# Residual rows written by a scatter in stage one and loaded per block; the order of GpSimd's scatters

## The chip, the core and the metric

One core of a Trainium2 chip. The metric is the device time of one launch, in microseconds (us). TensorE (PE) multiplies, VectorE (DVE) and ScalarE (ACT) work on tiles, GpSimd (POOL) does small tiles and issues the indirect DMAs, and SyncE (SP) issues the plain DMAs from its own queue. Every engine runs its own list in order and waits on semaphores.

## What is computed

x has 8 sequences of 2048 tokens with 256 features, 16384 tokens in all.

```
x = x + layernorm(attention(layernorm(x)))     # RWKV: k, v, r projections, a log-space scan, output product
h2 = layernorm(x)
x = x + layernorm(moe(h2))                     # 8 experts, the best 2 of each token, plus a shared expert
```

`moe` weighs the two routed experts' outputs by the softmax of their logits and adds the shared expert's output, gated by a sigmoid. The last line needs three things for each token: the sum of its expert outputs, its shared expert's row, and the residual x as it stood before the experts.

## The kernel before

**Stage one** runs over NCH = 32 chunks of 512 tokens (NT = 4 tiles of 128 rows). The chunks go through a software pipeline that is written out by hand: every engine has a loop over i, and in turn i it handles chunk i in one function, chunk i-1 in the next, down to chunk i-6. What matters here, by chunk m:

- ACT, in its turn m+3, at the end: `squares_o(m)` (L731) and, later in the same turn, `squares_h2(m)` (L742), which need `residual(m)` of DVE (L1014).
- ACT, in its turn m+4: `h2_normed(m)` (L715) writes the normalised rows h2n. It waits for `scale_h2(m)` (L527) of POOL, which makes rstd and nb.
- PE, in its turn m+3, at the end: `T2(m)` transposes h2n. In its turn m+4 it does the output product of chunk m+1, `router_product(m)` and `gate_up_product(m)`; ACT's `gate(m)` (L770) evacuates the latter.
- ACT, in its turn m+5, as the last thing of the turn: `shared_out(m)` (L665) writes the shared expert's rows `ysh`.
- POOL, in its turn i: `scale_o(i-4)`, `scatter(i-5, 0)` and `scatter(i-5, 1)` (four indirect DMAs each, from h2n to the DRAM tensors d_xd0 and d_xd1, sorted by expert), `scale_h2(i-4)`, `scale_in(i)`, and last `shared_scatter(i-6)` (L554, four indirect DMAs, from ysh to d_xs). So the rows of `shared_out(m)` leave in POOL's turn m+6, at its end.

A scattered row carries, beside its 256 features, the weights, positions and token number, and in two more columns (`ext`) the factor and the mean from which the residual can be had back from the normalised row.

**Between the stages** SP writes zero blocks (`tails`, `shared_tails`, `tail_2`) behind the last row of every expert in each scattered tensor, DVE computes the block tables, and the last scatters land.

**Stage two** runs over 142 blocks of 256 rows, 71 for the first choice of each token and 71 for the second. SP loads the block (`load_block`) and, LY = 5 steps later, the result rows to add to (`load_result`: d_xs in the first half, d_ys in the second). PE transposes and multiplies, ACT and DVE split operands into high and low parts, DVE adds in `y_out` (L1327). In the first half POOL scatters the sums to d_ys. In the second half `back` (L1336) recomputes the residual on DVE from the block, `last_squares` (ACT, L887) and `last_scale` (POOL, L594) make the last norm's factor, `final` (DVE, L1345) puts them together and `tokens_out` (POOL, L605) scatters the rows to `out`.

POOL's order in stage one is this:

```
if on(i - 4): scale_o(i - 4)
if on(i - 5): scatter(i - 5, 0); scatter(i - 5, 1)
if on(i - 4) and i - 4 != NCH - 1: scale_h2(i - 4)
if 0 < i < NCH: scale_in(i)
if on(i - 6): shared_scatter(i - 6)
```

Of the kernel before, what the change touches and what calls it, by code (L numbers as in the profile page):

```python
# [14 lines left out]
P = 128  # L15
# [9 lines left out]
def rwkv_moe(nc, x, decay, u_in, mix_k, mix_v, mix_r, wkT, wvT, wrT, woT, router, w1, w2,  # L25
# [18 lines left out]
    NEXT = XW - C_EXT  # L44
# [6 lines left out]
    LY = 5  # L51
# [7 lines left out]
    d_xs = nc.dram_tensor("d_xs", [E * CAP + BLK, D], F32).ap()  # L59

    d_ys = nc.dram_tensor("d_ys", [E * CAP + BLK, D], F32).ap()

    with ExitStack() as ctx:
# [41 lines left out]
        x1 = sb("x1", [P, NT, D])  # L105
# [4 lines left out]
        lowf = sb("lowf", [P, P])  # L110
# [13 lines left out]
        sqo = sb("sqo", [P, 2, 2, D], BF16)  # L124
# [22 lines left out]
        ext = sb("ext", [P, 2, NT, NEXT])  # L147
# [12 lines left out]
        ioti = sb("ioti", [P, NBP], I32)  # L160
# [48 lines left out]
        s_ex = sem("s_ex")  # L209
        s_exc = sem("s_exc")  # L210
# [55 lines left out]
        s_zt = sem("s_zt")  # L266
        s_tb = sem("s_tb")
# [26 lines left out]
        s_back = sem("s_back")  # L294
# [17 lines left out]
        def rows(t):  # L312
# [11 lines left out]
              for i in range(2) for t in (kk, vv, tr, dl, nx, x1)]  # L324
# [8 lines left out]
        tbf = flat(hf)[:, 0:4 * NBP].rearrange("p (k s b) -> p k s b", k=2, s=2)  # L333
        stf = st[:, :, :, :].rearrange("p k a t -> p (k a t)")
# [4 lines left out]
        bigj = [t[:, 0:E * NJ].rearrange("p (e b) -> p e b", e=E) for t in room]  # L339

# [16 lines left out]
        def _(sp):  # L357
# [20 lines left out]
            def tails():  # L378

                sp.wait_ge(s_zt, 2)  # L380
                for s in range(2):
                    sp.dma_start(d_xd[s][E * CAP:E * CAP + BLK, :].rearrange("(p j) d -> p j d", p=P), zt
                                 ).then_inc(s_tail, 16)
                sp.dma_start(d_xs[E * CAP:E * CAP + BLK, :].rearrange("(p j) d -> p j d", p=P), zt[:, :, 0:D]
# [21 lines left out]
            sp.dma_start(x1[:, :, :], x_v[0]).then_inc(s_xr, 16)  # L406
            for i in range(NCH + 4):
# [18 lines left out]
            sp.wait_ge(s_tail, 16 * (E + 2))  # L426
# [3 lines left out]
            def load_block(b):  # L430
# [4 lines left out]
                first_row[b % (LY + 1)] = r  # L435
# [3 lines left out]
            def load_result(w):  # L439
# [4 lines left out]
                sp.dma_start(yb[w % NYB], rows_in[bass.ds(first_row[w % (LY + 1)], BLK), :].rearrange("(p j) d -> p j d", p=P)  # L444
                             ).then_inc(s_yl[w % NYB], 16)

            for b in range(NB + LY):
                if b == NB1:
                    sp.wait_ge(s_tab, 5)
                    sp.wait_ge(s_tail2, 16 * E)  # L450
# [6 lines left out]
                if b >= LY:  # L457
                    if b == LY:
                        sp.wait_ge(s_scy, 16 * NT * NCH)
                        sp.wait_ge(s_tail3, 16 * (E + 1))  # L460
                    if b - LY == NB1:
                        sp.wait_ge(s_tail4, 16 * (E + 1))
                        for w in range(NB1 - NYB, NB1):
                            sp.wait_ge(*landed(w))
                    load_result(b - LY)
# [5 lines left out]
        def _(pool):  # L471
            g = nc.gpsimd
            g.memset(ident[:, :], 0.0).then_inc(s_const, 1)
            g.memset(lowf[:, :], 1.0).then_inc(s_const, 1)
# [3 lines left out]
            g.affine_select(out=lowf[:, :], in_=lowf[:, :], compare_op=ALU.is_gt, fill=0.0,  # L478
# [5 lines left out]
            g.memset(ext[:, :, :, :], 0.0).then_inc(s_const, 1)  # L484
            g.memset(oneb[:, :], 1.0).then_inc(s_const, 1)
            g.memset(ones8[:, :], 1.0).then_inc(s_const, 1)
            g.iota(ioti[:, :], [[1, NBP]], base=0, channel_multiplier=0).then_inc(s_const, 1)
# [21 lines left out]
            def scale_in(c):  # L509
                if c:  # L510
                    pool.wait_ge(s_nx, n(c - 1, NT, NT))
                if c >= 4:
# [3 lines left out]
                    pool.wait_ge(s_ex, n(c - 4, 2, 2))  # L516
# [10 lines left out]
            def scale_h2(m):  # L527
# [8 lines left out]
                if m >= 2:  # L536
                    pool.wait_ge(s_exc, m - 1)
                g.tensor_tensor(ext[:, m % 2, :, 0], var[:, 2, :], rstd[:, 2, :], ALU.mult).then_inc(s_ex, 1)
                g.tensor_copy(ext[:, m % 2, :, 1], nmx[:, m % 4, :]).then_inc(s_ex, 1)

            def scatter(m, s):
                if s == 0:
                    pool.wait_ge(s_h2, n(m, NT, NT))
                    pool.wait_ge(s_ex, n(m, 2, 2))
                    g.tensor_copy(h2n_of(m)[:, :, C_EXT:XW], ext[:, m % 2, :, :]).then_inc(s_exc, 1)
                    pool.wait_ge(s_exc, m + 1)
                pool.wait_ge(s_pl, n(m, NPL, L_DST))
                pool.wait_ge(s_wt, n(m, NWT, W_CW))
                for j in range(NT):
                    k = s * NT + j  # L550
                    g.indirect_dma_start(d_xd[s], bass.IndirectOffsetOnAxis(ap=ixs[:, m % 2, k:k + 1], axis=0),  # L551
                                         h2n_of(m)[:, j, :], None).then_inc(s_sct, 16)

            def shared_scatter(m):  # L554
                pool.wait_ge(s_pl, n(m, NPL, L_IX))
                for j in range(NT):
                    pool.wait_ge(s_ys, n(m, NT, j + 1))
                    g.indirect_dma_start(d_xs, bass.IndirectOffsetOnAxis(ap=ixs[:, m % 2, j:j + 1], axis=0),  # L558
# [3 lines left out]
            for i in range(NCH + 6):  # L562
# [9 lines left out]
                if i - 4 == NCH - 1:  # L572
                    scale_h2(i - 4)
                if on(i - 5):
# [6 lines left out]
                if on(i - 6):  # L581
                    shared_scatter(i - 6)
# [39 lines left out]
        def _(act):  # L622
# [92 lines left out]
            def h2_normed(m):  # L715
# [8 lines left out]
                for j in range(NT):  # L724
                    A.activation(h2n_of(m)[:, j, 0:D], x1[:, j, :], ACT.Identity, bias=nb[:, 2, j:j + 1],
# [5 lines left out]
            def squares_o(m):  # L731


                if m:
                    act.wait_ge(s_va[1], m)
                for j in range(NT):
                    act.wait_ge(s_O, n(m, 2, j // 2 + 1))
                    if n(m, NT, j) >= 2:
                        act.wait_ge(s_sqo, n(m, NT, j) - 1)
                    A.activation(sqo[:, 0, j % 2, :], o_tile(j), ACT.Square, accum_out=sq[:, 0, j:j + 1]).then_inc(s_sqo, 1)  # L740
# [900 lines left out]
```

## Time and profile before

| | us |
|---|---|
| median of 3 runs | 1677.63 (1674.99 to 1678.86) |
| the profiled execution | 1681.43 |
| its span, first to last instruction | 1679.7 |

Busy shares over the span, from the page: PE 91%, DVE 84%, ACT 78%, POOL 66%. The granted clock's mean is 0.964. The slices of the page:

```profile
PE   4899999999999999999999996669999988888882
POOL 1156677677677677677667767535666647777776
PEclk9999999999999999999999998779999999999997
DMA  3113223222222222222322211389877745665561
```

Each digit is a fortieth of the span, 42 us. Stage one fills slices 1 to 26, stage two the rest. The busy time of a matmul is modelled, so "PE busy" tells that PE was never without work, not that it was at its peak. In the rows of a timeline, the bracket at the end is how long the engine was idle before the row, and what released it; "issue" is time for which the profile shows no release. A row may merge several equal instructions (x4).

### The profile page before, as it was taken

Reading aid. Unit: us, or ns where it says so; the run is one execution under the profiler, and the core shown is the slowest. Engines: PE = TensorE matmul, PEld = TensorE weight load, DVE = VectorE, ACT = ScalarE, POOL = GpSimd, SP = SyncE. Lnnn points to the kernel's source line nnn. Section 1 sums busy time; section 2 is a strip of 40 time slices with the busy share of each in tenths; the row PEclk is TensorE's granted clock in tenths of the full one; section 3 lists DMA queues with packets and bytes.
Section 4 is the critical chain, followed back from the end, with each engine's and each line's share of the span. In section 5 each row is a group of like instructions: output and inputs, shape, how many; then the busy total and the mean of one; then the engine's idle time right before and its main releaser. Section 6 shows DMA issues by size and latency. Waiting matters only on the chain.

```text
span 1679.7 us, 35120 instructions
## 1 busy us (share of the span) xinstructions
PE 1532.7 (91%) x9960; PEld 1373.8 (82%) x9960; DVE 1407.1 (84%) x3210; ACT 1314.1 (78%) x2699; POOL 1103.0 (66%) x1167
## 2 busy tenths in 40 slices
PE   4899999999999999999999996669999988888882
PEld 3778888888888888888888885668999988878872
DVE  4799998998998898899899888547777769999994
ACT  3788888898898898888898888545777767777772
POOL 1156677677677677677667767535666647777776
PEclk9999999999999999999999998779999999999997
DMA  3113223222222222222322211389877745665561
GB/s 119 39 52 92 98 82 101 98 85 93 91 85 84 87 85 84 91 82 76 102 80 77 90 66 66 111 263 294 253 238 245 240 155 162 200 213 174 185 206 62
DMA packets 122316, 214.42 MB, mean 128 GB/s; under 512 B 19975, under 2 KB 62730, under 8 KB 122128
## 3 DMA queue, kind: packets, MB, share of 16 engines
q1 hardware_dynamic: 90064, 126.13, 25.2%
q0 software_dynamic: 32064, 86.04, 14.1%
q8 instruction: 86, 1.41, 0.4%
q14 instruction: 102, 0.84, 0.2%
HBM read 116.37 MB, written 99.39 MB: 128 GB/s over the span
## 4 chain that ended last, share of the span: by engine, by line
PE 66%; POOL 7%; DVE 7%; issue 7%; DMA 4%; SPq 2%; ACT 2%; DVEq 1%; POOLq 0%; ACTq 0%
PE PS L1401 47%; PE PS L1581 6%; PE PS L1597 5%; PE PS L1393 3%; POOL out L609 2%; PE PS L1464 2%; POOL d_ys L591 2%; POOL d_xd L551 2%; PE PS L1462 2%; PE PS L1562 1%; SPq L434 1%; SPq L436 0%; DMA kk<-d_ys 0%; POOL rsw L603 0%; DVE ysh L1342 0%
## 5 line engine op out<-in xcount | busy, mean ns | idle before, releaser
L551 POOL DMA_INDIRECT d_xd<-h2n,ixs x248 | 309.4, 1248 | 192.7 <-DVE h2n L1153 124.7
L1401 PE MATMUL PS<-hTh,wqh 128*128 128x512 f32 x768 | 307.0, 400 | 16.2 <-ACT kk L646 11.0
L1401 PE MATMUL PS<-hTl,wqh 128*128 128x512 f32 x768 | 306.3, 399 | 0.0
L1401 PE MATMUL PS<-hTh,wql 128*128 128x512 f32 x768 | 306.3, 399 | 0.0
L1401 PEld LDWEIGHTS PS<-hTh,wqh 128*128 128x128 f32 x768 | 146.7, 191 | 51.0 <-ACT kk L646 11.8
L1401 PEld LDWEIGHTS PS<-hTh,wql 128*128 128x128 f32 x768 | 146.3, 190 | 34.5
L1401 PEld LDWEIGHTS PS<-hTl,wqh 128*128 128x128 f32 x768 | 146.7, 191 | 33.4
L558 POOL DMA_INDIRECT d_xs<-ysh,ixs x124 | 132.5, 1069 | 43.6 <-issue 43.2
L1581 PE MATMUL PS<-rkh 128*128 128x256 f32 x284 | 87.6, 308 | 27.1 <-DVE rkl L1373 25.0
L1597 PE MATMUL PS<-weh,h2h 128*128 x380 | 106.9, 281 | 0.0
L1597 PE MATMUL PS<-weh,h2l 128*128 x380 | 106.8, 281 | 0.0
L1597 PE MATMUL PS<-wel,h2h 128*128 x380 | 106.7, 281 | 0.0
L1401 PE MATMUL PS<-h2h,wgh 128*128 128x512 f32 x256 | 106.7, 417 | 0.0
L1581 PE MATMUL PS<-hTh,shh 128*128 128x256 f32 x284 | 87.0, 306 | 18.2 <-DVE shl L1373 15.9
L1379 DVE TENSOR_TENSOR h2l<-al,h2h 128x512 fp32r<-128x512 f32 x95 | 65.1, 685 | 43.6 <-ACT h2h L917 43.5
L1401 PE MATMUL PS<-h2l,wgh 128*128 128x512 f32 x256 | 101.2, 395 | 0.0
L1401 PE MATMUL PS<-h2h,wgl 128*128 128x512 f32 x256 | 100.8, 394 | 0.0
L913 ACT ACTIVATE al<-PS 128x512 f32<-128x512 f32 x95 | 56.8, 598 | 55.0 <-PE PS L1581 54.1
L502 POOL TENSOR_SCALAR var<-mv 128x4 f32<-128x4 f32 x32 | 29.6, 926 | 85.7 <-DVE mv L980 85.1
L1581 PEld LDWEIGHTS PS<-rkh 128*128 128x128 f32 x284 | 55.6, 196 | 34.1 <-issue 21.3
L1581 PE MATMUL PS<-rkh,rkl 128*128 128x256 f32 x284 | 82.1, 289 | 0.0
L1581 PE MATMUL PS<-rkl,rkh 128*128 128x256 f32 x284 | 82.0, 289 | 0.0
(308 smaller groups left out, 5777.8 us busy)
## 6 DMA issues: line engine op xcount, KB each, us to landing
xin<-in_L_attn_x SPq DMA_DIRECT2D x32, 512.0 KB, 4.3
x<-in_L_attn_x SPq DMA_DIRECT2D x32, 512.0 KB
wqh<-d_xd SPq DMA_DIRECT2D x60, 272.0 KB, 3.7
wql<-d_xd SPq DMA_DIRECT2D x60, 272.0 KB, 3.5
d_xd<-ee SPq DMA_DIRECT2D x18, 272.0 KB
wel<-in_L_ffn_w SPq DMA_DIRECT2D x16, 256.0 KB
d_xd<-h2n,ixs POOLq DMA_INDIRECT x248
kk<-d_xs SPq DMA_DIRECT2D x12, 256.0 KB, 3.6
```

The costliest lines, as they stand in the source:

```text
L551: g.indirect_dma_start(d_xd[s], bass.IndirectOffsetOnAxis(ap=ixs[:, m % 2, k:k + 1], axis=0), h2n_of(m)[:, j, :], None).then_inc(s_sct, 16)
L558: g.indirect_dma_start(d_xs, bass.IndirectOffsetOnAxis(ap=ixs[:, m % 2, j:j + 1], axis=0), ysh_of(m)[:, j, :], None).then_inc(s_scy, 16)
L591: g.indirect_dma_start(d_ys, rows_at(w, j, C_POS), yb[w % NYB][:, j, :], None, bounds_check=E * CAP - 1, oob_is_err=False).then_inc(s_yo[w ...
L609: g.indirect_dma_start(out_r, rows_at(w, j, C_TOK), yb[w % NYB][:, j, :], None, bounds_check=N - 1, oob_is_err=False).then_inc(s_yo[w % NY ...
L913: A.activation(sil[u % 3], hidB[u % 3][:, :], ACT.Silu).then_inc(s_sil, 1)
L1379: V.tensor_tensor(aTl[u % 3], sil[u % 3], aTh[u % 3].bitcast(F32), ALU.subtract).then_inc(s_al2, 1)
L1393: ins = nc.tensor.transpose(bank[a][:, j * P:(j + 1) * P], src[:, j, a * P:(a + 1) * P], ident[:, :])
L1401: ins = mm_(out_ap, l, r, start=(k == 0), stop=(k == len(todo) - 1))
L1462: mm_(both, h2h[:, a, at], rwp[:, a, :], start=(a == 0), stop=False)
L1464: ins = mm_(both[:, 0:RW], h2l[:, a, at], rwp[:, a, 0:RW], start=False, stop=(a == H - 1))
L1581: ins = mm_(hidB[u % 3][:, f * D:(f + 1) * D], l, r, start=(k == 0), stop=(k == len(todo) - 1))
L1597: ins = mm_(outB[w % 3][:, j * D:(j + 1) * D], l, r, start=(k == 0), stop=(k == len(todo) - 1))
```

## The change

The residual rows x1 are scattered to a new DRAM tensor d_x1 in stage one, at the places of the second choice, and loaded block by block in the second half of stage two; `back` and the two `ext` columns' arithmetic go. x1 becomes two buffers, the row numbers `ixs` three. POOL's `shared_scatter(i - 6)` moves from the end of its turn to the place behind `scale_o(i - 4)`, and the new `residual_scatter(i - 5)` stands at the end. SP writes zero tails to d_x1 too. `load_result` follows `load_block` by two steps instead of five (by up to six at the start of each half), and `load_residual` by seven. The order of ACT and PE doesn't change. To make room, `lowf` and `ioti` move into hf, and the two squares of ACT share one output tile.

```diff
-    LY = 5
+    LY = 2
+    LT = 6
+    LX = 7
+    d_x1 = nc.dram_tensor("d_x1", [E * CAP + BLK, D], F32).ap()
-        x1 = sb("x1", [P, NT, D])
+        x1 = sb("x1", [P, 2, NT, D])
-        ixs = sb("ixs", [P, 2, 2 * NT], U32)
+        ixs = sb("ixs", [P, 3, 2 * NT], U32)
...
             def tail_2(e):
+                sp.dma_start(d_x1[bass.ds(r, BLK), :].rearrange("(p j) d -> p j d", p=P), zt[:, :, 0:D]).then_inc(s_tail2, 16)
...
                 if 0 < i - 3 < NCH:
-                    sp.wait_ge(s_h2, n(i - 3 - 1, NT, NT))
-                    sp.dma_start(x1[:, :, :], x_v[i - 3]).then_inc(s_xr, 16)
+                    if i - 3 >= 2:
+                        sp.wait_ge(s_scx, 16 * NT * (i - 4))
+                    sp.dma_start(x1_of(i - 3), x_v[i - 3]).then_inc(s_xr, 16)
...
+            def load_residual(v):
+                w = NB1 + v
+                if v >= 4:
+                    sp.wait_ge(s_fin, 2 * (v - 3))
+                sp.dma_start(xk[v % 4], d_x1[bass.ds(first_row[w % (LX + 1)], BLK), :].rearrange("(p j) d -> p j d", p=P)
+                             ).then_inc(s_x1l[v % 4], 16)
...
-            for b in range(NB + LY):
+            for b in range(NB + LX):
...
+                due = [b - LY] if LY <= b < NB + LY and (b - LY) % NB1 >= LT - LY else []
+                if b % NB1 == LT and b < NB:
+                    due = list(range(b - LT, b - LY + 1))
+                for w in due:
...
+                    load_result(w)
+                if b - LX >= NB1:
+                    load_residual(b - LX - NB1)
...
             def scale_h2(m):
...
-                if m >= 2:
-                    pool.wait_ge(s_exc, m - 1)
-                g.tensor_tensor(ext[:, m % 2, :, 0], var[:, 2, :], rstd[:, 2, :], ALU.mult).then_inc(s_ex, 1)
-                g.tensor_copy(ext[:, m % 2, :, 1], nmx[:, m % 4, :]).then_inc(s_ex, 1)
...
             def scatter(m, s):
                 if s == 0:
                     pool.wait_ge(s_h2, n(m, NT, NT))
-                    pool.wait_ge(s_ex, n(m, 2, 2))
-                    g.tensor_copy(h2n_of(m)[:, :, C_EXT:XW], ext[:, m % 2, :, :]).then_inc(s_exc, 1)
-                    pool.wait_ge(s_exc, m + 1)
...
+            def residual_scatter(m):
+                pool.wait_ge(s_x1, n(m, NT, NT))
+                pool.wait_ge(s_sqh, n(m, NT, NT))
+                pool.wait_ge(s_h2, n(m, NT, NT))
+                pool.wait_ge(s_pl, n(m, NPL, L_IX))
+                for j in range(NT):
+                    g.indirect_dma_start(d_x1, bass.IndirectOffsetOnAxis(ap=ixs[:, m % 3, NT + j:NT + j + 1], axis=0),
+                                         x1_of(m)[:, j, :], None).then_inc(s_scx, 16)
...
                     scale_o(i - 4)
                 if i - 4 == NCH - 1:
                     scale_h2(i - 4)
+                if on(i - 6):
+                    shared_scatter(i - 6)
                 if on(i - 5):
                     scatter(i - 5, 0)
                     scatter(i - 5, 1)
...
                     scale_h2(i - 4)
                 if 0 < i < NCH:
                     scale_in(i)
-                if on(i - 6):
-                    shared_scatter(i - 6)
+                if on(i - 5):
+                    residual_scatter(i - 5)
...
-                if m >= 2:
+                if m >= 3:
 
-                    dve.wait_ge(s_sct, 16 * 2 * NT * (m - 1))
-                    dve.wait_ge(s_scy, 16 * NT * (m - 1))
-                V.tensor_copy(ixs[:, m % 2, :], posa[:, :]).then_inc(s_pl, 1)
+                    dve.wait_ge(s_sct, 16 * 2 * NT * (m - 2))
+                    dve.wait_ge(s_scy, 16 * NT * (m - 2))
+                    dve.wait_ge(s_scx, 16 * NT * (m - 2))
+                V.tensor_copy(ixs[:, m % 3, :], posa[:, :]).then_inc(s_pl, 1)
...
-            def back(v):
-
-                w = NB1 + v
-                if v >= 4:
-                    dve.wait_ge(s_fin, 2 * (v - 3))
-                for j in range(2):
-                    V.tensor_scalar(xk[v % 4][:, j, :], xb[w % NX][:, j, 0:D], xb[w % NX][:, j, C_EXT:C_EXT + 1], xb[w % NX][:, j, C_EXT + 1:C_EXT + 2],
-                                    ALU.mult, ALU.subtract).then_inc(s_back, 1)
-
             def final(v):
                 w, q, k = NB1 + v, v // 2, v % 2
                 dve.wait_ge(s_rsw, q + 1)
-                dve.wait_ge(s_back, 2 * (v + 1))
+                dve.wait_ge(s_x1l[v % 4], 16 * (v // 4 + 1))
```

## Rows read from the trace of the kernel before


**Rows 1.** Windows: busy us (x) of PE, PEld, DVE, ACT, POOL; clock; DMA, GB/s.

```profile
400.00:600.00 200.00, 200.00 (x1163) 172.46 (x1162) 183.33 (x415) 178.22 (x361) 143.09 (x151) 1.00 0.26 86
1200.00:1300.00 100.00, 100.00 (x860) 100.00 (x858) 74.52 (x155) 72.96 (x123) 68.28 (x61) 1.00 0.78 248
...
1450.00:1500.00 50.00, 44.66 (x358) 41.95 (x357) 48.35 (x114) 38.76 (x104) 39.00 (x39) 1.00 0.60 191
```

**Rows 2.** Timeline of POOL in one turn: start, us, what, idle before.

```profile
581.75 1.06 POOL L545 COPY h2n<-ext 128x48 f32<-128x48 f32 x1
586.71 1.08 POOL L551 DMA_INDIRECT d_xd<-h2n,ixs  x1 [3.90 <-DVE h2n L1153]
...
599.03 0.40 POOL L531 TENSOR_SCALAR var<-sq 128x4 f32<-128x4 f32 x1
...
606.85 1.10 POOL L558 DMA_INDIRECT d_xs<-ysh,ixs  x1 [0.47 <-issue]
...
612.30 0.19 POOL L523 TENSOR_SCALAR var<-sq 128x4 f32<-128x4 f32 x1 [0.45 <-ACT sqo L740]
```

**Rows 3.** Timeline of ACT over the same turn and into the next.

```profile
592.39 1.54 ACT L671 ACTIVATE ysh<-PS,ssum 128x256 f32<-128x256 f32 x4
...
602.01 2.08 ACT L725 ACTIVATE h2n<-x,nb,rstd 128x256 f32<-128x256 f32 x4 [0.16 <-POOL nb L535]
...
605.13 0.59 ACT L654 COPY vv<-PS 128x512 f32<-128x512 f32 x1 [0.56 <-PE PS L1401]
606.51 1.07 ACT L761 CAST h2h<-PS 128x512 fp32r<-128x512 f32 x2 [0.80 <-PE PS L1393]
...
612.94 0.60 ACT L775 ACTIVATE hf<-PS 128x512 f32<-128x512 f32 x1 [0.73 <-PE PS L1401]
...
624.22 1.54 ACT L671 ACTIVATE ysh<-PS,ssum 128x256 f32<-128x256 f32 x4
```

**Rows 4.** Timeline of PE, the transposes of h2n in that turn.

```profile
605.80 1.04 PE L1393 MATMUL PS<-ident,h2n 128*128 128x128 f32 x8
```

**Rows 5.** Source L671 (shared_out): duration ns min/median/max, first and last start.

```profile
L671 ACT ACTIVATE ysh<-PS,ssum x124: 449/458/474, 146.8 to 1096.0; 128x256 f32<-128x256 f32 x124
```

**Rows 6.** Source L551: the same for the scatters to d_xd.

```profile
L551 POOL DMA_INDIRECT d_xd<-h2n,ixs x248: 956/962/2007, 111.0 to 1078.7; - x124
```

**Rows 7.** Windows round an idle stretch of PE near stage one's end.

```profile
1038.00:1040.00 2.00, 0.00 (x0) 0.00 (x0) 2.00 (x3) 2.00 (x5) 1.39 (x3) 0.50 0.30 102
...
1048.00:1050.00 2.00, 0.77 (x4) 0.80 (x5) 2.00 (x3) 1.08 (x3) 1.82 (x2) 0.50 0.00 0
...
1054.00:1056.00 2.00, 2.00 (x16) 2.00 (x15) 2.00 (x2) 0.88 (x5) 1.69 (x3) 0.76 0.20 72
```

**Rows 8.** Groups by line, 1400 to 1640: x count | busy, mean ns.

```profile
L1371 DVE TENSOR_TENSOR rkl<-PS,rkh 128x512 fp32r<-128x512 f32 x29 | 19.7, 679 | 0.0
...
L1342 DVE TENSOR_SCALAR ysh<-wqh 128x256 f32<-128x256 f32 x30 | 11.3, 418 | 0.0
```

**Rows 9.** Timeline of DVE in stage two's second half.

```profile
1562.09 0.84 DVE L1342 TENSOR_SCALAR xin<-wgh 128x256 f32<-128x256 f32 x2
1562.86 0.87 DVE L1351 SCALAR_TENSOR_TENSOR vv<-vv,rsw,ysh 128x256 f32<-128x256 f32 x2
```

**Rows 10.** Timeline of POOL in the same stretch, two blocks apart.

```profile
1560.16 1.06 POOL L609 DMA_INDIRECT out<-x,wql  x1 [0.20 <-issue]
...
1566.65 1.07 POOL L609 DMA_INDIRECT out<-vv,wql  x1 [0.20 <-issue]
```

**Rows 11.** Timeline of SP: the first block load and the first result load.

```profile
1105.07 1.63 SPq L436 DMA_DIRECT2D wqh<-d_xd  x2
...
1124.83 0.42 SPq L444 DMA_DIRECT2D kk<-d_xs  x1
```

**Rows 12.** Timeline of SP: the load of x1 in a turn of stage one.

```profile
604.12 0.37 SPq L421 DMA_DIRECT2D x<-in_L_attn_x  x1
```

**Rows 13.** Timeline of DVE: the use of x1 one turn earlier, in residual.

```profile
585.84 1.66 DVE L1019 SCALAR_TENSOR_TENSOR x<-PS,rstd,x 128x256 f32<-128x256 f32 x4
```

More of the change, by code:

```diff
@@ L293, in rwkv_moe @@
         s_rsw = sem("s_rsw")
-        s_back = sem("s_back")
+        s_scx = sem("s_scx")
+        s_x1l = [sem(f"s_x1l{i}") for i in range(4)]
         s_fin = sem("s_fin")
@@ L323, in rwkv_moe @@
         yb = [flat(t)[:, i * 2 * D:(i + 1) * 2 * D].rearrange("p (j d) -> p j d", j=2)
-              for i in range(2) for t in (kk, vv, tr, dl, nx, x1)]
+              for i in range(2) for t in (kk, vv, tr, dl, nx)]
+        x1f = x1[:, :, :, :].rearrange("p k j d -> p (k j d)")
+        yb += [x1f[:, i * 2 * D:(i + 1) * 2 * D].rearrange("p (j d) -> p j d", j=2) for i in range(2)]
         assert len(xb) == NX and len(yb) == NYB
@@ L477, in _ @@
                             base=0, pattern=[[-1, P]], channel_multiplier=1).then_inc(s_const, 1)
-            g.affine_select(out=lowf[:, :], in_=lowf[:, :], compare_op=ALU.is_gt, fill=0.0,
+            g.affine_select(out=lowf, in_=lowf, compare_op=ALU.is_gt, fill=0.0,
                             base=0, pattern=[[1, P]], channel_multiplier=-1).then_inc(s_const, 1)
@@ L483, in _ @@
             g.memset(mh4[:, :], -0.5).then_inc(s_const, 1)
-            g.memset(ext[:, :, :, :], 0.0).then_inc(s_const, 1)
+            g.memset(h2n[:, :, C_EXT:XW], 0.0).then_inc(s_const, 1)
             g.memset(oneb[:, :], 1.0).then_inc(s_const, 1)
             g.memset(ones8[:, :], 1.0).then_inc(s_const, 1)
-            g.iota(ioti[:, :], [[1, NBP]], base=0, channel_multiplier=0).then_inc(s_const, 1)
+            g.iota(ioti, [[1, NBP]], base=0, channel_multiplier=0).then_inc(s_const, 1)
             g.iota(toki[:, :], [[P, NT]], base=0, channel_multiplier=1).then_inc(s_const, 1)
@@ L724, in h2_normed @@
                 for j in range(NT):
-                    A.activation(h2n_of(m)[:, j, 0:D], x1[:, j, :], ACT.Identity, bias=nb[:, 2, j:j + 1],
+                    A.activation(h2n_of(m)[:, j, 0:D], x1_of(m)[:, j, :], ACT.Identity, bias=nb[:, 2, j:j + 1],
                                  scale=rstd[:, 2, j:j + 1]).then_inc(s_h2, 1)
@@ L748, in squares_h2 @@
                 for j in range(NT):
[L749 removed]
+                    if j >= 2:
                         act.wait_ge(s_sqh, n(m, NT, j) - 1)
[L751 removed]
+                    A.activation(sqo[:, j % 2, :], x1_of(m)[:, j, :], ACT.Square, bias=nmx[:, m % 4, j:j + 1],
                                  accum_out=sq[:, 1, j:j + 1]).then_inc(s_sqh, 1)
@@ L809, in _ @@
             act.wait_ge(s_const, NCONST)
-            copy(lowb[:, :], lowf[:, :]).then_inc(s_aprep, 1)
+            copy(lowb[:, :], lowf).then_inc(s_aprep, 1)
             high_mix(0, al)
@@ L816, in _ @@
             act.wait_ge(s_tmp, 14)
-            copy(all_of(woh), x1[:, 0:2, :].rearrange("p j d -> p (j d)")).then_inc(s_wh, 1)
+            copy(woh[:, :, :], x1_of(0)[:, 0:2, :]).then_inc(s_wh, 1)
             act.wait_ge(s_wld[2], 16)
@@ L894, in last_squares @@
                         act.wait_ge(s_sqw, 2 * v + j - 1)
-                    A.activation(sqo[:, 0, j, :], yb[w % NYB][:, j, :], ACT.Square,
+                    A.activation(sqo[:, j, :], yb[w % NYB][:, j, :], ACT.Square,
                                  accum_out=sqw[:, q % NPR, 2 * k + j:2 * k + j + 1]).then_inc(s_sqw, 1)
@@ L1018, in residual @@
                 for j in range(NT):
-                    V.scalar_tensor_tensor(out=x1[:, j, :], in0=o_tile(j), scalar=rstd[:, 1, j:j + 1],
-                                           in1=x1[:, j, :], op0=ALU.mult, op1=ALU.add).then_inc(s_x1, 1)
+                    V.scalar_tensor_tensor(out=x1_of(m)[:, j, :], in0=o_tile(j), scalar=rstd[:, 1, j:j + 1],
+                                           in1=x1_of(m)[:, j, :], op0=ALU.mult, op1=ALU.add).then_inc(s_x1, 1)
             def sums(i):
@@ L1381, in _ @@
                     y_out(t - 3)
-                if 0 <= t - 3 - NB1 < NB1:
-                    back(t - 3 - NB1)
                 if t - 6 >= NB1:
```

65 lines of the change are left out of this document (35 added, 30 removed).

## The prediction

> **What bounds the kernel now.** I read the stages first, then the places of waits. The windows [rows 1] show PE busy 200 of 200 us in stage one and 100 of 100 in stage two's first half: there PE sets the pace, and DVE (183 of 200) and ACT (178) only just keep up. In the second half PE drops to 44.7 of 50 and DVE rises to 48.4: there DVE sets the pace. So DVE work that is removed from the second half can pay, and in stage one a change is free as long as PE never starves.
>
> One turn of stage one lasts 31.83 us, from one `shared_out` on ACT at 592.39 to the next at 624.22 [rows 3]. What the change moves is POOL's order, so POOL's turn is the second thing to read [rows 2]. POOL finishes `scale_o` at 581.75 and sits idle 3.90 us until DVE has the weights, scatters eight times from 586.71 to 599.03, does `scale_h2`, then `scale_in`, and from 606.85 the four shared scatters; its next turn begins at 612.30. ACT's `h2_normed` starts at 602.01, and it had waited 0.16 us for the last result of `scale_h2` [rows 3]. PE takes the transposes of these rows at 605.80 [rows 4]. So `scale_h2` has almost no slack on ACT, and some 1.6 us on PE (605.80 less the end of h2n, 604.09, and about 0.1 of handover).
>
> **The change, part by part.**
>
> *The shared scatters at the front of POOL's turn.* This is the part that decides. Which rows do they need? POOL's turn i scatters the rows of chunk i-6, and ACT writes these in `shared_out(i-6)`, the last function of its turn i-1. `scale_o(i-4)`, the step ahead of it on POOL, needs `squares_o(i-4)`, which lies in the middle of the same turn of ACT. In times of the trace: POOL is through with `scale_o` at 581.75 [rows 2], but the rows of this turn's shared scatters are begun at 592.39 [rows 3]. That they are the same rows follows from the tile: there is one `ysh`, and ACT may not write it at 592.39 before the last turn's scatters landed. Before, the scatters stood at 606.85 and the rows were long there. At the front, POOL waits from 581.75 for about 11 us, and behind it on POOL's list stand the eight scatters, `scale_h2`, `scale_in` and the four new scatters. Waiting for `scale_h2` are ACT's `h2_normed`, and through it PE's transposes, router and gate products, ACT's `gate` and all that follows on ACT to the next `shared_out`, which releases POOL's next turn. This is a ring through both engines that is closed once in a turn, and before the change it wasn't there. Its length is the new turn, if it is longer than 31.83 us:
>
> - From the start of `shared_out` to h2n: the first of its four instructions, 0.46 us [rows 5]; an issue gap of 0.47 as before the shared scatters now; four shared scatters, 606.85 to 612.30 less the 0.45 idle, 5.0; and from the first scatter to h2n as now, 586.71 to 602.01, 15.3, with 0.1 between. The two small `ext` instructions stand behind the result that ACT waits for, so their removal saves nothing here. Sum 21.4 us, where it is 602.01 - 592.39 = 9.6 now: 11.8 more.
> - From h2n to the next `shared_out`: 624.22 - 602.01 = 22.2 now. PE will be idle and take the rows at once, which saves the 1.6. But it stands idle some 10 us ahead of them, and the windows at the end of stage one show what an idle stretch does [rows 7]: with no matmul from 1034 to 1049 the granted clock is at 0.50, the lower level, from the window at 1038 on, and when PE begins at about 1049.2 (0.77 us of work in that window) it stays there until the window at 1054, whose mean of 0.76 puts the rise at about 1055.0. That is 5.7 us at half speed, 2.9 us lost, and just on the products that `gate` waits for: ACT waits for PE there already (0.73) [rows 3]. Sum 22.2 - 1.6 + 2.9 = 23.5.
>
> The ring is 44.9 us, 13.1 us over 31.83. It acts in the turns of POOL in which a shared scatter stands ahead of a `scale_h2` that follows it, i = 6 to 34, 29 of them (the last chunk's `scale_h2` is ahead of it): 11.8 for the first and 28 x 13.1, **+379 us**.
>
> Both ends of this term: the scatters take 956 to 2007 ns, most at 962 [rows 6]; with all eight at their least and a gap of 0.3 they take 10.1 of the present 12.3, 2.2 less. On ACT the waits for PE of 0.56, 0.80 and 0.73 [rows 3] could all go, and the lower clock cost nothing: 22.2 - 2.1 = 20.1. The shortest ring is 19.2 + 20.1 = 39.3, +7.5 a turn, +215 us. Upwards, half speed for a whole ten us instead of 5.7 would add 2.2 a turn, +61.
>
> On the scatters' length, VectorE's load may count. The Trainium skill (GPSIMD Engine Reference, Specifications) says that GpSimd shares its SBUF interfaces with VectorE and contends with VectorE instructions that have two SBUF inputs. By that rule the long scatters get rarer in a turn in which DVE is busy two thirds of the time instead of 92%; if half of the excess went, the sum would be some 30 us less. The trace shows long and short scatters, and not what makes them long.
>
> *The four residual scatters.* POOL gets 4 more per turn (5.1 us at the shared ones' pace) and loses the `ext` copies. They stand where the shared ones stood, and in a turn of 44.9 us POOL's work of about 31 (its 30.5 now, 612.30 - 581.75, less 3.9 idle, plus 5.1) fits. Zero. If the order cost nothing they would fill the idle 3.9 us and the `ext` copy's 1.06, and fit just so.
>
> *x1's load* now waits for the residual scatters of two chunks before instead of for h2n, on SP's queue, with xin's next load behind it. Now it is issued at 604.12 [rows 12], 2.1 us after h2n's start, and used by DVE 585.84 + 31.83 = 617.67 [rows 13]. The scatters will end 10 us after h2n's start (`scale_in` 3.4 and a gap, then 5.1), land about 2 later, and the load takes 4.3 (page, issues): there at 16.4 us, used at 15.7 + 1.3 = 17.0. So 0.6 us are left; zero, but a second ring lies close under it. xin has 20 us to spare.
>
> *The border of the stages.* The last shared scatters and the eight of the last chunk stand in the other order, and the chunk's scatters end up to 10 us later; the first block load, at 1105.07 [rows 11], waits for them and for zero blocks and tables, so I take 5 of the 10. Nine more zero blocks of 256 KB go out at a time when the DMA engines are full: 248 GB/s at a share of 0.78 make 318 GB/s at the full share [rows 1], 7.4 us. The first result load slips one step behind (1124.83 now [rows 11]). Together +12, between 4 and 22.
>
> *Second half of stage two.* 29 of every second block in 240 us [rows 8] are 4.14 us a block. `back` takes two instructions of 418 ns [rows 8], in sequence 0.77 (1562.09 to 1562.86) [rows 9]. Without it DVE is at 3.4 or less. What is late next: PE, 3.25 us a block at full rate (1.00 clock, its first-half pace), POOL, which does two blocks in 6.49 us where nothing holds it [rows 10], 3.25 each, but 39.0 of 50 us busy now, 3.2, with 0.3 of issue ahead of each scatter, 3.8; and the DMA engines: 191 GB/s x 4.14 = 790 KB a block now, plus 262, at 318 GB/s 3.3 us. Three limits within 0.5 us don't mesh perfectly: I take 3.6, a gain of 0.54 on 66 steady blocks, **-36 us**; between 3.8 and 3.3, -22 to -56. The results' earlier loads are within this.
>
> Sum against the profiled execution's 1681.4 us: + 379 + 12 - 36 = 2036; it lay 3.8 above the median, so 2033.
>
> **The rivals.**
>
> *The ring at its short end* (slower still): PE's waits vanish, the scatters are short, the clock doesn't matter. 1677.6 + 215 + 12 - 36 = 1869; a middle course, 1930 to 1960. For it: the scatters' median is at the low end; against it: the clock's rows, and PE's products lie on ACT's path already.
>
> *Faster.* The shared rows are ready at the front after all, because POOL runs so far behind ACT that the wait is none. It decides at the point where POOL leaves `scale_o` later than ACT ends `shared_out`: 581.75 against 592.85 now, so POOL would have to be 11 us late without PE feeling it, and PE has 1.6. Then stage one keeps 31.83 us a turn and the time is 1677.6 + 12 - 36 = 1654. The only thing for it is that the pieces fit POOL's idle time so neatly.
>
> *A longer ring through x1.* The residual scatters' landing or the load takes 3 us more than I allow, and DVE's `residual`, the squares and `shared_out` move by 2.4: 28 x 2.4 on top, 2100.
>
> **How the numbers follow.** Forecast 0.74; short or middle ring 0.12; longer ring 0.07; faster 0.06; no change 0.01. Predicted 2033. Within the forecast, the clock's +61, the scatters' -60 and the small terms' 20 give 1965 to 2095; to hold 8 in 10 with the neighbours I take 1930 to 2090. A measurement tells about 0.2% from no change. Faster 0.06, same 0.01, slower 0.93.
>
> **What would show it.** In POOL's turn, a wait for ysh of about 11 us before the first shared scatter, and none for DVE's weights after it. Starts of `shared_out` some 45 us apart. ACT idle some 12 us for nb ahead of h2n; PE idle some 10 us ahead of the transposes of h2n, and matmuls at the lower clock for 5 us after. In stage two's second half, no wait of DVE for d_ys, blocks 3.6 us apart, a DMA share near 0.9. I am wrong if POOL's wait for ysh is short, if turns stay at 32 us, or if ACT's gap ahead of h2n isn't there.

## The result, and the profile after

The changed kernel takes **2004.7 us** (median of 4 runs, 2000.4 to 2006.8) against 1677.1 before (4 runs): a ratio of 1.195, 95% interval 1.193 to 1.197. It is slower by 327 us; 2033 were forecast, 1930 to 2090 as the range. The profiled execution took 2006.8, its span 2005.0 (before 1681.4 and 1679.7).

The page of the kernel after, each digit a fortieth of the span (50 us):

```profile
PE   4897767887877788876778777774569999999893
POOL 1255555445555544555554555545636666488876
PEclk8998888988898889888889888886779999999997
DMA  3122222222222221122222122122399777588884
```

PE's row had nines through all of stage one; now it has mostly sevens and eights, at a granted clock of 0.8 to 0.9, and stage one reaches to slice 28. In stage two PE's row is fuller than before. Two windows, with the columns of [rows 1]:

```profile
400.00:600.00 200.00, 159.40 (x860) 137.27 (x856) 139.10 (x313) 130.34 (x260) 103.10 (x111) 0.91 0.22 77
...
1780.00:1830.00 50.00, 46.94 (x388) 45.49 (x388) 45.81 (x100) 43.72 (x112) 41.32 (x43) 1.00 0.90 296
```

In stage one no engine is busy for more than 160 of 200 us. That is the mark of a ring: when everybody has idle time, read the waits and not the loads. One turn of POOL, to be held against [rows 2]:

```profile
702.11 1.04 POOL L547 TENSOR_TENSOR rstd<-var,mhalf 128x4 f32<-128x4 f32 x1
716.36 1.79 POOL L587 DMA_INDIRECT d_xs<-ysh,ixs  x1 [13.21 <-ACT ysh L702]
...
723.36 1.01 POOL L571 DMA_INDIRECT d_xd<-h2n,ixs  x1 [0.30 <-issue]
...
733.95 0.19 POOL L553 TENSOR_SCALAR var<-sq 128x4 f32<-128x4 f32 x1
734.22 1.04 POOL L555 TENSOR_TENSOR rstd<-var,mhalf 128x4 f32<-128x4 f32 x1
...
738.64 1.08 POOL L580 DMA_INDIRECT d_x<-x,ixs  x1 [0.91 <-issue]
```

ACT in the same turn, against [rows 3], and PE, against [rows 4]:

```profile
715.12 1.53 ACT L702 ACTIVATE ysh<-PS,ssum 128x256 f32<-128x256 f32 x4
735.65 2.07 ACT L756 ACTIVATE h2n<-x,nb,rstd 128x256 f32<-128x256 f32 x4 [10.98 <-POOL nb L557]
758.92 1.53 ACT L702 ACTIVATE ysh<-PS,ssum 128x256 f32<-128x256 f32 x4
...
737.87 1.94 PE L1417 MATMUL PS<-ident,h2n 128*128 128x128 f32 x8 [9.19 <-ACT h2n L756]
```

POOL is through with `scale_o` at 703.15 and waits 13.2 us for rows that ACT begins at 715.12; ACT waits 11.0 us for POOL's nb. The turn is 758.92 - 715.12 = 43.8 us where it was 31.8. The waits added up over 400 to 1300 us (us in total, times, longest) show that it is so in every turn:

```profile
POOL d_xs L587 <- ACT ysh L702: 276.5, 21, 13.5
ACT h2n L756 <- POOL nb L557: 236.9, 21, 12.2
...
PE PS L1417 <- ACT h2n L756: 187.3, 20, 10.3
```

The granted clock falls while PE is idle and comes back late; windows of 2 us in the same turn (PE's busy time is the second figure, the clock the third from the end):

```profile
732.00:734.00 2.00, 0.00 (x0) 0.00 (x0) 0.00 (x0) 0.00 (x0) 1.62 (x3) 0.83 0.31 115
734.00:736.00 2.00, 0.00 (x0) 0.00 (x0) 0.00 (x0) 0.35 (x1) 1.59 (x4) 0.50 0.22 70
...
740.00:742.00 2.00, 2.00 (x12) 2.00 (x11) 1.88 (x5) 1.97 (x5) 1.67 (x2) 0.50 0.36 131
742.00:744.00 2.00, 2.00 (x13) 2.00 (x13) 1.75 (x3) 2.00 (x7) 1.68 (x2) 0.61 0.18 66
744.00:746.00 2.00, 2.00 (x21) 2.00 (x20) 0.00 (x0) 1.16 (x6) 0.60 (x2) 1.00 0.18 66
```

The span's 325.3 us more are made up of: stage one's steady turns, from the third h2n (156.4 before, 168.1 after) to the thirty-first (1047.0, 1389.8), 28 turns of 43.6 in place of 31.8, +331.1; the turns ahead of them +11.7; from there to the first block load (1105.1, 1455.1) +7.2; stage two's first half 266.9, then 270.8, +3.9; its second half 307.7, then 279.0, -28.7. (This is one profile of each kernel; that of the kernel before lies 4 us over its median.) The halves meet where DVE first adds to a row of d_ys (1372.0 before, 1726.0 after).

### The profile page after: what moved, and what is told of

Read it like the earlier page. It is cut to its first block, busy times and chain, and to the rows that moved or that the text cites. A ratio compares the mean times of both kernels' runs of the same rounds, so it can differ in the third digit from the quotient of the medians.

```text
span 2005.0 us, 35201 instructions
## 1 busy us (share of the span) xinstructions
PE 1581.5 (79%) x9960; PEld 1423.9 (71%) x9960; DVE 1365.9 (68%) x3068; ACT 1317.8 (66%) x2699; POOL 1107.0 (55%) x1200
## 4 chain that ended last, share of the span: by engine, by line
PE 27%; POOL 25%; issue 18%; ACT 16%; DMA 5%; DVE 2%; SPq 2%; DVEq 0%; ACTq 0%; POOLq 0%
POOL d_xd L571 12%; PE PS L1425 12%; POOL d_xs L587 6%; PE PS L1605 4%; PE PS L1621 4%; POOL out L640 3%; PE PS L1417 3%; ACT h2n L756 3%; ACT sqo L784 2%; ACT al L721 2%; ACT L903 2%; ACT ee L729 2%; ACT be L710 2%; ACT ysh L702 2%; POOL rstd L555 2%
## 5 line engine op out<-in xcount | busy, mean ns | idle before, releaser
L587 POOL DMA_INDIRECT d_xs<-ysh,ixs x124 | 188.1, 1517 | 417.5 <-ACT ysh L702 388.5
L571 POOL DMA_INDIRECT d_xd<-h2n,ixs x248 | 258.2, 1041 | 80.5 <-issue 75.3
L1417 PE MATMUL PS<-ident,h2n 128*128 128x128 f32 x248 | 58.4, 414 | 297.7 <-ACT h2n L756 297.7
L756 ACT ACTIVATE h2n<-x,nb,rstd 128x256 f32<-128x256 f32 x124 | 64.2, 588 | 329.7 <-POOL nb L557 329.7
L1117 DVE TENSOR_TENSOR h2l<-PS,h2h 128x512 fp32r<-128x512 f32 x64 | 44.0, 691 | 323.6 <-ACT h2h L794 321.1
L1417 PEld LDWEIGHTS PS<-ident,h2n 128*128 128x128 f32 x248 | 47.2, 218 | 304.3 <-issue 302.2
L580 POOL DMA_INDIRECT d_x<-x,ixs x128 | 127.9, 999 | 50.1 <-issue 50.1
L1425 PE MATMUL PS<-woh,rkh 128*128 128x256 f32 x256 | 94.6, 370 | 1.7 <-DVE rkl L1206 1.7
```

The costliest lines, as they stand in the source:

```text
L580: g.indirect_dma_start(d_x1, bass.IndirectOffsetOnAxis(ap=ixs[:, m % 3, NT + j:NT + j + 1], axis=0), x1_of(m)[:, j, :], None).then_inc(s_s ...
L756: A.activation(h2n_of(m)[:, j, 0:D], x1_of(m)[:, j, :], ACT.Identity, bias=nb[:, 2, j:j + 1], scale=rstd[:, 2, j:j + 1]).then_inc(s_h2, 1)
L1117: V.tensor_tensor(h2l[:, a, :], pT2[a][:, :], h2h[:, a, :].bitcast(F32), ALU.subtract).then_inc(s_h2l, 1)
L1417: ins = nc.tensor.transpose(bank[a][:, j * P:(j + 1) * P], src[:, j, a * P:(a + 1) * P], ident[:, :])
L1425: ins = mm_(out_ap, l, r, start=(k == 0), stop=(k == len(todo) - 1))
```

## Experiments

### The order of POOL's turn

The first run takes the changed kernel and puts only the shared scatters back.

```diff
@@ POOL's turn, kernel after
-                if on(i - 6):
-                    shared_scatter(i - 6)
                 if on(i - 5):
                     scatter(i - 5, 0)
...
                     scale_in(i)
+                if on(i - 6):
+                    shared_scatter(i - 6)
                 if on(i - 5):
                     residual_scatter(i - 5)
```

> The changed kernel, with one edit: POOL's shared_scatter(i-6) stands again behind scale_in, just ahead of residual_scatter(i-5). Theory A (the ring through the shared rows makes the loss): the ring is open again, POOL's turn is 31.8 to 32.1 us of work, stage one is back at 31.8 to 32.2 us a turn, and the rest of the change stays (border and first half +11 us, second half -29 us): 1655 to 1675 us. Theory B (the loss comes from POOL's 16 scatters a turn, or from x1's load that waits for them): all of these are still there, and the time stays above 1900 us.

**1808.3 us**, ratio 1.079 (1.075 to 1.083): neither of the two. 196 us of the 327 go with the order, but a turn is 37.0 us and not 31.8 (turns are here and below the mean of 28, from the third h2n to the thirty-first). The waits over 400 to 1000 us name other culprits than in the kernel after:

```profile
POOL var L525 <- DVE mv L1014: 128.8, 16, 9.4
DVE x L1053 <- DMA x<-in_L_attn_x: 105.8, 16, 7.5
```

and a turn of SP, DVE and POOL shows how they hang together:

```profile
697.40 0.37 SPq L431 DMA_DIRECT2D x<-in_L_attn_x  x1
...
701.95 1.66 DVE L1053 SCALAR_TENSOR_TENSOR x<-PS,rstd,x 128x256 f32<-128x256 f32 x4 [6.23 <-DMA x<-in_L_attn_x]
...
718.74 1.02 POOL L525 TENSOR_SCALAR var<-mv 128x4 f32<-128x4 f32 x1 [5.78 <-DVE mv L1014]
...
734.49 0.37 SPq L431 DMA_DIRECT2D x<-in_L_attn_x  x1
```

x1's load waits for the residual scatters to land. DVE's `residual` waits for the load; `stats_in`, which stands behind it in DVE's turn, ends at 718.6; POOL's `scale_in` waits for that, and behind `scale_in` stand the shared and then the residual scatters, which end at 733.0. Load 4.6, DVE's turn 16.8, POOL 14.3, landing 1.4: 37.1 us in this turn. It is the second ring of which the prediction said that it lies close by. In the kernel after it is hidden: there x1 lands 2.7 us before DVE uses it, on the mean of 18 turns, and never less than 1.4.

If that is the ring, the shared scatters need only change places with the residual ones:

```diff
@@ POOL's turn, on top of the run before
-                if on(i - 6):
-                    shared_scatter(i - 6)
                 if on(i - 5):
                     residual_scatter(i - 5)
+                if on(i - 6):
+                    shared_scatter(i - 6)
```

> The run before this one with the old order (e1) took 37 us a turn, and its trace shows DVE's residual waiting 6.1 us for x1's load. Edit here: e1 with the two last scatters of POOL's turn exchanged, residual_scatter(i-5) ahead of shared_scatter(i-6). Theory C (a second ring: residual on DVE, stats, scale_in, shared scatters, residual scatters, their landing, x1's load, residual): the ring loses the shared scatters' 5.1 us and is 31.8 to 32.3 us, as long as PE's work: 1655 to 1685 us. Theory D (POOL's 16 scatters a turn are too much work, or the DMA queues are): the same work in another order, so the time stays within 20 us of e1's 1808.

**1706.0 us**, ratio 1.019 (1.017 to 1.020). 102 us from the exchange of two neighbours, so the ring is shown; the time is 21 us above its range. A turn is still 33.4 us, and DVE's `residual` waits no more for the load but for POOL:

```profile
DVE x L1053 <- POOL rstd L547: 53.2, 16, 4.8
```

The reading is that POOL is late because it got mv late. To try it, `stats_in(i)` went ahead of `denominator(i - 3)` in DVE's turn:

```diff
@@ DVE's turn, on top of the run before
                     weighed_sums(i - 3)
+                if 0 < i < NCH:
+                    stats_in(i)
+                if on(i - 3):
                     denominator(i - 3)
...
                     receptance(i - 3)
-                if 0 < i < NCH:
-                    stats_in(i)
```

> The same as e5_residual_first, with DVE's stats_in(i) moved ahead of denominator(i-3), 5 to 6 us earlier in DVE's turn, so that POOL's scale_in no longer waits for it. If e5's turn is still over 31.83 us because of the second ring, this takes the rest of it: e5 less 0 to 12 us. If DVE's later denominator and what follows it (1.8 us later) starve PE, it is slower than e5 by up to 50 us.

**1679.8 us**, ratio 1.004 (1.002 to 1.006), 26 us less than the run before where 0 to 12 were expected. Turns are 32.3 us, the wait above fell to 8.5 us, and the window shows who is left:

```profile
400.00:600.00 200.00, 198.05 (x1165) 170.16 (x1164) 178.21 (x427) 173.65 (x351) 162.16 (x154) 1.00 0.31 107
```

POOL is busy 162 of 200 us, 26.3 a turn, and 16 scatters have 0.3 us of issue ahead of them, 4.8: 31.1 of 32.3. With the residual scatters a turn is thus 0.5 us longer than before even in the best order found. That POOL sets this turn is likely, but no run here takes work off it to show it.

### The front alone, the wait alone

Two runs build on the kernel before. One moves the shared scatters to the front and changes nothing else; the other leaves them in place and adds only their wait at the front.

```diff
@@ POOL's turn, kernel before, first run
+                if on(i - 6):
+                    shared_scatter(i - 6)
                 if on(i - 5):
                     scatter(i - 5, 0)
...
                     scale_in(i)
-                if on(i - 6):
-                    shared_scatter(i - 6)
@@ POOL's turn, kernel before, second run
+                if on(i - 6):
+                    pool.wait_ge(s_ys, n(i - 6, NT, 1))
                 if on(i - 5):
                     scatter(i - 5, 0)
```

> The kernel before, with one edit: shared_scatter(i-6) moved from the end of POOL's turn to the place behind scale_o(i-4). No residual scatter, no new loads. Theory A: the same ring, 43 to 44.5 us a turn, so 335 to 365 us on the kernel before: 2010 to 2040 us. Theory B: POOL has its 12 scatters a turn as before, so within 10 us of the kernel before.

**2034.8 us**, ratio 1.214 (1.211 to 1.217), as expected; turns of 44.0 us. The front alone makes the whole loss, and the rest of the change gives some 30 us back.

> The kernel before, with one added wait: behind scale_o(i-4) POOL waits for the first shared row tile of chunk i-6, and the shared scatters stay where they were, at the end of the turn. Theory A: a ring without the four scatters' 6.9 us and without a part of the lower clock's loss, 35.5 to 37 us a turn: 105 to 150 us on the kernel before, 1785 to 1830 us. If the place of the four scatters alone made the loss, and not the wait, it stays at 1677 us.

**1849.8 us**, ratio 1.104 (1.100 to 1.107), 20 above the range. The two large waits over 400 to 1000 us:

```profile
POOL h2n L545 <- ACT ysh L673: 191.6, 16, 12.8
ACT h2n L727 <- POOL nb L535: 96.9, 16, 7.5
```

A turn is 37.7 us. That is the ring of the kernel after, 43.6, less its shared scatters (716.36 to 723.36, 7.0) and plus the `ext` copy, 1.06, which now stands behind the wait too: 37.7. The turn is 0.7 us over the expected 35.5 to 37, and 28 times that is the 20 us. Half of the loss, then, is the wait, and half is that the scatters stand inside the ring behind it.

### The clock

The kernel after, with 34 matmuls of 512 columns, their result thrown away, put ahead of the transposes of h2n in 26 turns, so that PE is busy while it would wait:

```diff
@@ PE's turn, kernel after
+                    if 6 <= i < NCH:
+                        wide = wqh[:, 0, :, :, :].rearrange("p s a n -> p (s a n)")
+                        for _ in range(34):
+                            mm_(pT2[0][:, :], wide[:, 0:P], wide[:, 0:TC], start=True, stop=True)
                     T2(i - 3, 0)
```

> The changed kernel, with 34 matmuls of 512 columns added ahead of the transposes of h2n in turns 6 to 31 of PE, into the bank that the transposes overwrite: about 8 us of work where PE is idle 9.2. They keep PE at the higher clock and change nothing of the result. Theory A with the clock as a term of the ring (2.9 us a turn): the matmuls behind the transposes are back at full speed, the ring is 40.5 to 41.5 us, 55 to 80 us less than the changed kernel: 1925 to 1950 us. If ACT's own work hides the lower clock, the time stays within 10 us of the changed kernel's 2005.

**1949.9 us**, ratio 1.163 (1.160 to 1.167), just inside the range. With more work the kernel is 54.8 us faster, 2.1 for each of the 26 turns; 2.9 were priced. The window shows the clock near its upper level:

```profile
400.00:600.00 200.00, 192.27 (x1069) 163.65 (x1068) 139.44 (x337) 132.14 (x268) 109.81 (x124) 0.99 0.24 84
```

The clock's place in the ring is the wait of ACT's `gate` for PE's products, in a turn of the kernel after and in one of this run:

```profile
747.63 0.60 ACT L808 ACTIVATE hf<-PS 128x512 f32<-128x512 f32 x1 [2.40 <-PE PS L1425]
...
714.89 0.60 ACT L808 ACTIVATE hf<-PS 128x512 f32<-128x512 f32 x1 [0.71 <-PE PS L1425]
```

From h2n to that `gate` it is 11.5 us on the mean of 20 turns of the kernel after. In this run it is 9.3 us in 15 turns of 20; in the other five the clock had fallen all the same (to a mean of 0.83 in the ten us from 1 us before h2n's start) and it is 10.9. From `gate` to the next `shared_out` both have 11.3. So the lower clock costs the ring 2.2 us a turn.

### Stage two: early loads and residual rows apart

One run gives the kernel before the change's order of result loads alone; another takes it from the run with the residual scatters first.

```diff
@@ kernel before, first run; SP's loop then as in the change
-    LY = 5
+    LY = 2
+    LT = 6
+    LX = 7
@@ run with the residual scatters first, second run
-    LY = 2
-    LT = 6
+    LY = 5
+    LT = 5
```

> The kernel before, with the order of the result loads of the change (two steps behind the rows, the first ones in a batch) and nothing else. If DVE's waits for d_ys in the second half (13 us in the 240 us shown, of the kernel before) are time lost, 10 to 18 us less: 1660 to 1668 us; if the batch at the start of the first half costs what it seemed to (+4 us), 1664 to 1672. If DVE only waits somewhere else instead, within 3 us of the kernel before.

**1663.1 us**, ratio 0.992 (0.991 to 0.994), 13.5 us less than the kernel before and inside the first range: faster than both kernels. The run with the residual rows in their best order, 1679.8, has these early loads in it too and is 17 us slower. So the idea of the change, to load the residual rows instead of computing them, didn't pay in any order tried; the early loads alone did.

> The same as e5_residual_first, with LY = LT = 5, the result loads of the kernel before. What the earlier result loads are worth beside the removed DVE work: if POOL sets the pace of the second half, the late loads still cost their waits now and then, 3 to 15 us more than e5; if they cost as before, 13 to 20 us more; nothing, if POOL covers them.

**1733.2 us**, ratio 1.034 (1.033 to 1.036), 27 us over its twin; 3 to 20 were expected. Each half of stage two from its own profile, us:

| result loads | residual rows | first half | second half |
|---|---|---|---|
| late | computed (before) | 266.9 | 307.7 |
| early | computed | 266.4 | 290.4 |
| late | loaded | 275.9 | 300.4 |
| early | loaded, residual first | 271.5 | 277.0 |

The last row's twin with early statistics has 277.0 too: its span of 1677.0 less the second of these rows, where its second half begins (the first is where its first half does):

```profile
1127.61 1.49 SPq L446 DMA_DIRECT2D wqh<-d_xd  x2
...
1399.97 0.88 DVE L1369 SCALAR_TENSOR_TENSOR x<-PS,wgl,x 128x256 f32<-128x256 f32 x2 [5.57 <-DMA x<-d_ys]
```

How far one profile can be trusted here: the runs with the front alone and the wait alone have the stage two of the kernel before, unchanged, and in their profiles the second half takes 301.6 and 303.4 us, not 307.7. With the residual rows computed, the early loads thus give 11 to 17 us (the medians say 13.5 for the whole kernel); with the rows loaded they give 23. The residual rows give 1 to 7 us with late loads, which is not clear of that spread, and 13 with early ones. So the early loads need neither the residual rows nor anything of stage one, while the residual rows clearly pay only with the early loads. The new zero blocks and loads cost the first half 4 to 9 us. With late loads and loaded residual rows DVE waits for rows of d_ys 38 times in the second half, 48.7 us in sum; with early loads one such wait is left, 5.8 us, at the start of the half. It is the lateness of these loads, then, that holds DVE there.

### What makes POOL's instructions long

DVE is idle for 10.5 us ahead of its wait for h2h in the kernel after, just beside POOL's scatters and `scale_h2`. Two runs fill that time: one with eight additions of 128x1024, both inputs in SBUF, the other with 28 `bn_stats` of 128x256, one input each. The inputs are weights; the results go to `dl`, which is free there, and nothing uses them.

```diff
@@ DVE's turn, kernel after, first run
+                if 6 <= i < NCH:
+                    for _ in range(8):
+                        V.tensor_tensor(dl[:, :, :].rearrange("p a n -> p (a n)"),
...
+                                        ALU.add).then_inc(s_spare, 1)
+                        spared += 1
+                        dve.wait_ge(s_spare, spared)
                 if on(i - 4):
                     h2_low(i - 4)
@@ the same place, second run
+                if 6 <= i < NCH:
+                    for _ in range(7):
+                        for q in range(4):
+                            V.bn_stats(dl[:, 0, 6 * q:6 * q + 6], wqh[:, 0, q // 2, q % 2, :].bitcast(F32)).then_inc(s_spare, 1)
+                            spared += 1
+                        dve.wait_ge(s_spare, spared)
                 if on(i - 4):
                     h2_low(i - 4)
```

> The changed kernel with eight additions of 128x1024 (both inputs in SBUF, result thrown away, 1.2 us each) put on DVE ahead of its wait for h2h in turns 6 to 31. In the trace of the changed kernel DVE stands idle there for 10.5 us (729.2 to 739.7), while POOL issues the last of the eight scatters (0.96 us each), the power (1.04 us) and nb, and ACT waits for nb. The additions fill that idle time and nothing that the ring needs is queued behind them before 739.7, so by the queue alone they cost 0. Theory A: a POOL instruction that meets a DVE instruction with two inputs in SBUF runs longer, as the rows suggest (scatters of 1.3 to 2.0 us in place of 0.96, the power 2.03 to 2.10 in place of 1.04, wherever DVE runs such instructions beside them). Then four scatters gain 0.3 to 1.0 us each and scale_h2 1.3 us, the ring 2.5 to 5.3 us a turn, 26 turns: 2070 to 2145 us. Theory B: the long scatters are a coincidence or come from the traffic of the DMA queues, and DVE has no part: 2000 to 2015 us, as without the additions.

> The same place and about the same DVE time, but filled with 28 bn_stats of 128x256 (one input in SBUF, 0.35 us each) in place of the eight additions; results thrown away. In the trace of the changed kernel a scatter beside four bn_stats took 1.01 us and the next ones, beside a subtraction with two inputs and a scan, 1.34 and 1.24. If A holds in the form that two inputs are what counts: 2000 to 2015 us, scatters of 0.96 us. If any busy DVE lengthens POOL's instructions (A in the wider form): as the run with the additions, 2070 us or more. Under B: 2000 to 2015 us as well.

**2024.9 us** (ratio 1.208, 1.204 to 1.212) and **2003.7 us** (1.195, 1.193 to 1.197). The groups of POOL by form over 400 to 1300 us (busy, mean ns) of the first run, then of the second; L556 is the power of `scale_h2`, L526 the first step of `scale_in`, which adds a constant to 128x4 numbers:

```profile
L572 POOL DMA_INDIRECT d_xd<-h2n,ixs x160 | 167.0, 1044 | 48.8 <-issue 48.8
L556 POOL TENSOR_TENSOR rstd<-var,mhalf 128x4 f32<-128x4 f32 x20 | 40.5, 2027 | 1.7
L526 POOL TENSOR_SCALAR var<-mv 128x4 f32<-128x4 f32 x20 | 21.0, 1052 | 4.9 <-POOL nb L558 4.9
```

```profile
L572 POOL DMA_INDIRECT d_xd<-h2n,ixs x168 | 173.8, 1035 | 51.2 <-issue 51.2
L556 POOL TENSOR_TENSOR rstd<-var,mhalf 128x4 f32<-128x4 f32 x21 | 21.8, 1039 | 1.8
L526 POOL TENSOR_SCALAR var<-mv 128x4 f32<-128x4 f32 x20 | 4.9, 246 | 4.9 <-POOL nb L558 4.9
```

DVE was busy for 10.0 us at this place in both. With two inputs the power takes 2.03 us in place of 1.04 and the addition of 128x4 1.05 in place of 0.25; with one input they are as in the kernel after. The direction was right and the size was not: 20 us where 65 to 138 were expected, since the eight scatters hardly changed (1044 ns on average against 1035; one of the 160 took 2.04 us).

These additions don't speak for every DVE instruction, though. The shared scatters, which the change moved next to DVE's scans, take 1.52 us on average in the page of the kernel after and 1.07 in the page before. In 10 of the 21 turns between 400 and 1300 us the first of them takes 4.1 us, and in the other 11 the longest takes 1.8 to 2.1. One such turn, POOL and then DVE:

```profile
583.48 4.10 POOL L587 DMA_INDIRECT d_xs<-ysh,ixs  x1 [13.00 <-ACT ysh L702]
...
584.29 1.20 DVE L1082 SCALAR_TENSOR_TENSOR be<-ee,st 128x1024 f32<-128x1024 f32 x1
585.41 1.22 DVE L1091 SCALAR_TENSOR_TENSOR dl<-ee,vv 128x1024 f32<-128x1024 f32 x1
586.66 1.23 DVE L1097 TENSOR_TENSOR dl<-dl,st 128x1024 f32<-128x1024 f32 x1
```

Why a scatter is long beside these and not beside eight additions of the same size and about the same length, no run here shows. The eight routed scatters, which stood beside the scans before, went from 1.25 us on average to 1.04.

## Why the prediction was right

**The ring** was the right mechanism and carried the result: 44.9 us forecast, 43.6 measured, its term 379 forecast and 331 + 12 = 343 measured. In the turn shown it was 20.5 us from `shared_out` to h2n (735.65 - 715.12) for 21.4, and from h2n to the next `shared_out` 23.3 for 23.5; on the mean of 20 turns 20.6 and 22.8. The parts of the first piece were off both ways. In the turn shown the shared scatters took 7.0 us for 5.0, the eight scatters 10.6 for 12.3 and `scale_h2` 1.7 for 3.0. The last is explained by a run: with additions of two inputs beside it `scale_h2` takes 2.9 us again, with `bn_stats` 1.7. For the scatters the rows show only the company: the shared ones now stand beside the scans and the two-input instructions behind them, and the eight no longer do.

The Trainium skill's rule (GPSIMD Engine Reference, Specifications) that VectorE instructions with two SBUF inputs contend with GpSimd was weighed at some 30 us, for scatters that get shorter. The three differences are 2.0 - 1.7 - 1.3 = -1.0 a turn, 28 us, but that this comes so near is luck: the eight scatters alone gained 48, `scale_h2`, of which the prediction had said nothing, 36, and the shared scatters, to whose new neighbours the prediction did not apply the rule, lost 56. The pair of runs with one and two inputs agrees with the rule for POOL's own arithmetic; for the scatters it does not show it.

**The first turn** gave +11.7 for 11.8. The start of the steady part is where the ring first closes.

**The clock**: 5.7 us at half speed after PE's restart, at the end of stage one and in the middle of it (738 to 743.6) alike. It cost 2.2 us a turn, not 2.9: of the 2.9 us that PE loses, 2.2 reach ACT's `gate`. The other 0.7 most likely falls where ACT has work of its own, such as the copy of `vv` beside PE's transposes.

**Residual scatters at zero** was right only because the first ring left room. In the best order without it the turn is 0.5 us longer than before, and POOL has 31.1 of its 32.3 us filled.

**x1's load at zero** was right for this kernel, and with more room than the 0.6 us worked out: x1 lands 2.7 us before its use on the mean of 18 turns. The ring beneath it, named without a price of its own for the other order, is 37.0 us long as soon as the first is gone. Whoever undid only the front would have kept 131 of the 327 us.

**The border** and the first half came to +7.2 and +3.9, 11.1 for 12.

**The second half** gave 28.7 us for 36. Its new pace, 3.6 us a block, was right: 70 blocks in 254.7 us, 1733.0 to 1987.7 by the first and last start of POOL's `varw`, one for every two blocks. The step that failed is the pace before: "29 of every second block in 240 us" counts the ends of a window, and from the first to the last instruction it is 282.7 us for 70 blocks, 4.04 and not 4.14. 70 times 0.40 is 28. Even the 4.04 is one profile's: the two runs with the same stage two have 3.96 and 3.98. The gain was credited in the main to `back`'s removal; the runs show that the early loads alone make 11 to 17 us of it, and that without them loading the residual rows gives 1 to 7.

**The rivals**: the short end (1869) and the middle course (1930 to 1960) fall with turns of 43.6; the longer ring through x1 didn't show, x1 lands 2.7 us before DVE needs it; POOL's wait of 13.2 us rules out the faster one.

## What to carry to other kernels

When work moves on an engine's list, ask which instruction of another engine it needs and when that is issued in the same turn; if what stands behind it feeds that same engine, the move has closed a ring, and its length is read from two timelines. Removing one ring shows the next: here the turn went from 43.6 us to 37.0, 33.4 and 32.3, with 31.8 in the kernel before, and of what lay beneath the first ring only the next one had been named beforehand, and without a length. When work moves on an engine's list, ask also what the other engines run at its new place: the same four scatters took 7.0 us there and 5.0 at the old one. A change of several parts is worth taking apart even when it is slower as a whole, for here one part of it, the early result loads, makes the kernel before 0.8% faster.

## What the hardware showed

- POOL's small arithmetic is twice to four times as long beside DVE additions with two inputs in SBUF (the power 2.03 us for 1.04, an addition of 128x4 1.05 for 0.25) and untouched beside `bn_stats` (1.04 and 0.25).
- POOL takes 0.96 us for a scatter of 128 rows, and 0.30 pass before the next. Beside those additions the mean is 1.04 us, beside `bn_stats` 1.035, and one of 160 took 2.04 beside the additions. Beside a scan and the two-input instructions behind it the first shared scatter took 4.1 us in 10 turns of 21.
- In this kernel, where PE would idle for 9 us in a turn, 34 matmuls whose result nobody uses made it 2.7% faster, with the granted clock at 0.99 in place of 0.91.
